# Two nearest prototypes sought in the products, distances on ScalarE, and one load for the last keys' products

## The reference, cut to what matters

```
x = x + tanh(g_xattn[1]) * L1_xattn(layernorm(x), ctx)         # 16 heads, softmax over 77 keys
xf = layernorm(x)
d2 = |xf|^2 + |p|^2 - 2 * (xf @ prototypes.T)                  # 32 prototypes
dists = sqrt(max(d2, 0))
w = softmax(-dists / t);  topw, topi = top_k(w, 2);  topw = topw / sum(topw)
for slot in 0, 1:
    h = B[topi[slot]] @ xf                                     # rank 16
    out += topw[slot] * (A[topi[slot]] @ h + bias[topi[slot]])
x = x + tanh(g_ffn[1]) * out
```

## Time and profile before

| | us |
|---|---|
| median of 3 runs | 3044.14 |
| lowest, highest | 3039.18, 3046.79 |
| the profiled execution, its own time | 3044.48 |
| its span, first to last instruction | 3042.8 |
| PE busy | 2739.6 (90%) |
| DVE busy | 2507.4 (82%) |
| POOL busy | 2089.8 (69%) |
| ACT busy | 1983.7 (65%) |

### The profile page before, as it was taken

How to read it: one execution, slowest core, us unless ns; L and a number is a source line. 1 busy time by engine, 2 the same in 40 slices (tenths; PEclk the granted TensorE clock), 3 DMA queues, 4 the chain that set the end, 5 groups by cost and what they waited for, 6 DMA issues and landing times.

```text
span 3042.8 us, 96434 instructions
## 1 busy us (share of the span) xinstructions
PE 2739.6 (90%) x31534; PEld 2166.8 (71%) x31534; DVE 2507.4 (82%) x6126; ACT 1983.7 (65%) x4683; POOL 2089.8 (69%) x2777
## 2 busy tenths in 40 slices
PE   4888896899999999689699999999989999999996
PEld 2444444677777777557578888888878888888885
DVE  6877776688888888675689999899989989999885
ACT  2666666687777877575466666666656666666663
POOL 3893000567666676544388888888888888888886
PEclk9999998899999999899899999999999999999998
DMA  5987566223233232631567766666776767766663
GB/s 152 364 337 294 235 254 256 76 81 93 77 90 84 80 93 76 220 117 41 121 142 158 158 147 149 140 145 150 145 137 149 141 144 149 147 150 145 145 132 78
DMA packets 638943, 455.55 MB, mean 150 GB/s; under 512 B 389760, under 2 KB 612592, under 8 KB 633648
## 3 DMA queue, kind: packets, MB, share of 16 engines
q1 hardware_dynamic: 618288, 402.31, 52.2%
q0 software_dynamic: 7328, 23.40, 2.5%
q10 hardware_dynamic: 12960, 25.23, 2.2%
HBM read 235.08 MB, written 148.83 MB: 126 GB/s over the span
## 4 chain that ended last, share of the span: by engine, by line
PE 32%; DVE 6%; issue 4%; POOL 3%; SPq 2%; ACT 2%; DMA 1%; DVEq 0%; POOLq 0%; ACTq 0%
PE banks L150 10%; PE banks L152 9%; PE banks L151 9%; PE banks L1416 2%; DVE a_near L1540 2%; PE banks L1401 2%; SPq L1058 1%; DVE a_probT_lo L1492 1%; ACT a_qT_hi L1234 1%; DVE a_pick L1627 1%; DVE a_rsum L1504 1%; DVE a_wtop L1567 1%; POOL a_pn L1154 1%; DMA a_xnT<-a_xn_parts 0%; DMA a_hwT<-a_hw_parts 0%
## 5 line engine op out<-in xcount | busy, mean ns | idle before, releaser
L1234 ACT ACTIVATE a_qT_hi<-banks 128x512 f16<-128x512 f32 x252 | 150.4, 597 | 540.8 <-PE banks L152 540.8
L383 POOL TENSOR_TENSOR a_probT_lo<-a_expT,a_probT_hi 128x512 f16<-128x512 f32 x256 | 291.4, 1159 | 218.5 <-ACT a_probT_hi L466 218.5
L459 ACT ACTIVATE a_expT<-banks,a_top,w_score_scale 128x512 f32<-128x512 f32 (+1 forms) x384 | 272.4, 709 | 152.5 <-PE banks L550 146.1
L1154 POOL TENSOR_TENSOR a_pn<-a_prob,a_rsum 128x1024 f32<-128x1024 f32 (+1 forms) x256 | 310.2, 1233 | 5.8 <-DVE a_rsum L1506 5.8
L150 PE MATMUL banks<-a_xnT,w_q_hi 128*128 128x256 f16 x1024 | 281.2, 275 | 15.0 <-DMA a_xnT<-a_xn_parts 13.2
L150 PE MATMUL banks<-a_vo_front,a_probT_hi 128*128 128x256 f16 x1024 | 279.8, 273 | 9.4 <-DVE a_probT_lo L1492 6.5
L152 PE MATMUL banks<-a_xnT,w_q_lo 128*128 128x256 f16 x1024 | 280.6, 274 | 0.0
L151 PE MATMUL banks<-a_xnT,w_q_hi 128*128 128x256 f16 x1024 | 280.6, 274 | 0.0
L152 PE MATMUL banks<-a_vo_front,a_probT_lo 128*128 128x256 f16 x1024 | 279.7, 273 | 0.0
L151 PE MATMUL banks<-a_vo_front,a_probT_hi 128*128 128x256 f16 x1024 | 279.6, 273 | 0.0
L1490 DVE TENSOR_TENSOR a_qT_lo<-banks,a_qT_hi 128x512 f16<-128x512 f32 x252 | 172.0, 683 | 77.9 <-ACT a_qT_hi L1234 77.7
(11 more groups left out here) (380 smaller groups left out, 10177.7 us busy)
## 6 DMA issues: line engine op xcount, KB each, us to landing
vo<-kv_vo_out SPq DMA_DIRECT2D x38, 2048.0 KB, 8.1
a_vo_front<-vo SPq DMA_DIRECT2D x128, 512.0 KB
kt<-kv_k_out ACTq DMA_DIRECT2D x9, 2560.0 KB, 14.9
a_k<-kt SPq DMA_DIRECT2D x64, 308.0 KB, 3.5
kv_raw_e<-in_L_ffn_w POOLq DMA_DIRECT2D x16, 1024.0 KB, 8.9
a_x<-in_x SPq DMA_DIRECT2D x64, 256.0 KB, 2.9
a_y<-in_x SPq DMA_DIRECT2D x64, 256.0 KB, 2.7
x<-a_y SPq DMA_DIRECT2D x64, 256.0 KB, 2.8
```

The source lines that it names most:

```text
L383: pool.tensor_tensor(probT[b][1][:, first:end, :], expT[b][:, first:end, :], probT[b][0][:, first:end, :], ALU.subtract).then_inc(prob_rea ...
L459: act.activation(expT[1 - h][0:rows, first:end, :], bank, ACT.Exp, bias=top[0:rows, 0:1], scale=weights["score_scale"][0:rows, 0:1]).then_ ...
L1154: last = pool.tensor_tensor(keys_of(pn[h]), e[:, :, first:end], rsum[h][:, :].unsqueeze(2).broadcast_to([P, H, end - first]), ALU.mult)
L1234: act.activation(out, bank[:, 0:cols].rearrange("p (c s) -> p c s", c=out.shape[1]), ACT.Copy, scale=scale)\
```

## The change: what it does

Part 1, the search. The eight largest and their places are now sought in the products `dots` themselves, so `near` and its instruction go. One number is set (`idle_top`) ahead of the search, to stand for the waits. The squared distance of the two found is made on ACT by a new step, `square_gaps`: `square = Relu(ysq - top)` of two columns, placed after `probT` 0 (and the query piece behind it) in the next half. POOL's first step in `top_weights` adds `TINY` to it where it changed a sign before, and waits for ACT's result. `ysq` gets four columns, so that a length lives until it is used two halves later.

Part 2, the load. The last 13 keys' products of a batch come in one transfer of 104 partitions and not in eight of 13. The row order of `vo_back` is now key by key (key, then pair of heads) and not pair by pair. So the second instruction of `normalise` writes `pn` in that order: it reads `prob` with a step of 154 numbers in its innermost run of 8, where it read 13 neighbouring numbers before.

```diff
-    VALUE_LOADS = 16 * (2 + MAIN)
+    VALUE_LOADS = 16 * (2 + 1)
...
-            for n in range(MAIN):
-                sp.dma_start(vo_back[p][n * BACK:(n + 1) * BACK, :, :, :], values_back(batch_at(i), n)).then_inc(vo_in[p], 16)
+            sp.dma_start(vo_back[p][:, :, :, :], values_back(batch_at(i))).then_inc(vo_in[p], 16)
...
-            for keys_of, first, end in ((first_keys, 0, FRONT), (last_keys, FRONT, KEYS)):
-                last = pool.tensor_tensor(keys_of(pn[h]), e[:, :, first:end],
-                                          rsum[h][:, :].unsqueeze(2).broadcast_to([P, H, end - first]), ALU.mult)
-            last.then_inc(pn_ready, 1)
+            pool.tensor_tensor(first_keys(pn[h]), e[:, :, 0:FRONT],
+                               rsum[h][:, :].unsqueeze(2).broadcast_to([P, H, FRONT]), ALU.mult)
+            pool.tensor_tensor(last_by_key(pn[h]), e[:, :, FRONT:KEYS].rearrange("p (n a) k -> p a k n", a=2),
+                               rsum[h][:, :].rearrange("p (n a) -> p a n", a=2).unsqueeze(2)
+                               .broadcast_to([P, 2, BACK, MAIN]), ALU.mult).then_inc(pn_ready, 1)
...
-            need(pool, top_used, t)
-            pool.tensor_tensor(dist[:, :], top[:, 0:2], numbers[:, 2:3].broadcast_to([P, 2]), ALU.mult).then_inc(top_used, 1)
+            need(pool, gap_ready, t + 1)
+            kept = pool.tensor_tensor(dist[:, :], square[:, :], numbers[:, 2:3].broadcast_to([P, 2]), ALU.add)
             pool.tensor_copy(topf[:, :], topi[:, 0:2]).then_inc(top_ready, 1)
-            need(pool, top_used, t + 1)
+            step(kept)
...
+        def square_gaps(t, h, u):
+
+            n = (TPB * u + h - 6) % LENGTHS
+            need(act, top_found, t + 1)
+            need(act, ysq_done, t + 1)
+            need(act, more_ready, t)
+            act.activation(square[:, :], top[:, 0:2], ACT.Relu, bias=ysq[:, n:n + 1], scale=-1.0).then_inc(gap_ready, 1)
...
                     if g == 0:
                         prep(0)
+                        if live(t - 6, NT):
+                            square_gaps(t - 6, h, u)
...
-            need(act, near_ready, t - 1)
-            act.activation(ysq[:, h:h + 1], inv2[:, :], ACT.Identity, scale=mv2[:, 1:2]).then_inc(ysq_done, 1)
+            act.activation(ysq[:, n:n + 1], inv2[:, :], ACT.Identity, scale=mv2[:, 1:2]).then_inc(ysq_done, 1)
...
+            need(dve, gap_ready, t)
             need(dve, dots_read, t + 1)
-            need(dve, ysq_done, t + 1)
-            nc.vector.tensor_scalar(near[:, :], dots[:, :], ysq[:, 1 - h:2 - h], -TINY, ALU.subtract, ALU.min)\
-                .then_inc(near_ready, 1)
-            need(dve, top_used, t)
-            hold(near_ready, t + 1)
-            nc.vector.max(top[:, :], near[:, :]).then_inc(top_found, 1)
+            nc.vector.memset(idle_top[:, :], 0.0)
+            nc.vector.max(top[:, :], dots[:, :]).then_inc(top_found, 1)
```

More of the change, by code:

```diff
@@ L743, in attention_ffn_phase @@
     LU = 2
+    LENGTHS = 4
     LAG = 8
@@ L747, in attention_ffn_phase @@
     HALVES = ((0, 0), (0, 1), (1, 0))
-    SUM_STEPS, TOP_STEPS = 2, 3
+    SUM_STEPS, TOP_STEPS = 2, 4
     sb = lambda n, s, d=FP32: ctx.enter_context(nc.sbuf_tensor(f"{name}_{n}", s, d))
@@ L792, in attention_ffn_phase @@
         sem("yn_ready"))
-    ln_log, ln_root, more_ready, first_weight = sem("ln_log"), sem("ln_root"), sem("more_ready"), sem("first_weight")
+    gap_ready, ln_log, ln_root, more_ready, first_weight = sem("gap_ready"), sem("ln_log"), sem("ln_root"), sem("more_ready"), sem("first_weight")
     ln2_inverse = sem("ln2_inverse")
     yn_hi, yn_lo, dots_read = sem("yn_hi"), sem("yn_lo"), sem("dots_read")
-    near_ready, top_found, topi_found, top_ready = (
-        sem("near_ready"), sem("top_found"), sem("topi_found"), sem("top_ready"))
-    top_step, top_used, wtops_ready, picked, wsel_ready = (
-        sem("top_step"), sem("top_used"), sem("wtops_ready"), sem("picked"), sem("wsel_ready"))
+    top_found, topi_found, top_ready = sem("top_found"), sem("topi_found"), sem("top_ready")
+    top_step, wtops_ready, picked, wsel_ready = (
+        sem("top_step"), sem("wtops_ready"), sem("picked"), sem("wsel_ready"))
     low_ready, hw_ready, hw_hi, hw_lo, wselT_hi, wselT_ready, out_ready = (
@@ L875, in gpsimd_numbers @@
         def gpsimd_numbers(self):
-            for n, number in enumerate((-0.5, 0.5, -1.0, 1.0)):
+            for n, number in enumerate((-0.5, 0.5, TINY, 1.0)):
                 pool.memset(numbers[:, n:n + 1], number).then_inc(numbers_set, 1)
@@ L952, in attention_ffn_phase @@
     ynT = [sb(f"ynT{p}", [P, 2 * DC, P], F16) for p in range(2)]
-    ysq = sb("ysq", [P, TPB])
-    dots, near = sb("dots", [P, NPROTO]), sb("near", [P, NPROTO])
+    ysq = sb("ysq", [P, LENGTHS])
+    dots, idle_top = sb("dots", [P, NPROTO]), sb("idle_top", [P, 1])
     top, topi, topf = sb("top", [P, 8]), sb("topi", [P, 8], U32), sb("topf", [P, 2])
-    dist, dgap, late, wtop = sb("dist", [P, 2]), sb("dgap", [P, 1]), sb("late", [P, 1]), sb("wtop", [P, 2])
+    dist, square, dgap, late, wtop = sb("dist", [P, 2]), sb("square", [P, 2]), sb("dgap", [P, 1]), sb("late", [P, 1]), sb("wtop", [P, 2])
     more, euler, decay = sb("more", [P, 1]), sb("euler", [P, 1]), sb("decay", [P, 1])
@@ L1340, in body @@
                                    scale=rstd2[:, 0:1]).then_inc(yn_ready, 1)
-                    length2(t - 4, h)
+                    length2(t - 4, h, u)
                     normed_high(t - 4, u, h, j)
@@ L1528, in prototype_products @@
             bank = full(i, ("low", h, 0))
-            need(dve, near_ready, t)
+            need(dve, topi_found, t)
             need(dve, low_ready, t * LU + 1)
@@ L1534, in prototype_products, with nearest_two @@
                 .then_inc(dots_read, 1)
-        def nearest_two(t, h):
+        def nearest_two(t):
+            need(dve, gap_ready, t)
             need(dve, dots_read, t + 1)
-            need(dve, ysq_done, t + 1)
-            nc.vector.tensor_scalar(near[:, :], dots[:, :], ysq[:, 1 - h:2 - h], -TINY, ALU.subtract, ALU.min)\
-                .then_inc(near_ready, 1)
-            need(dve, top_used, t)
-            hold(near_ready, t + 1)
-            nc.vector.max(top[:, :], near[:, :]).then_inc(top_found, 1)
+            nc.vector.memset(idle_top[:, :], 0.0)
+            nc.vector.max(top[:, :], dots[:, :]).then_inc(top_found, 1)
         def nearest_index(t):
             hold(top_found, t + 1)
-            nc.vector.max_index(topi[:, :], top[:, :], near[:, :]).then_inc(topi_found, 1)
+            nc.vector.max_index(topi[:, :], top[:, :], dots[:, :]).then_inc(topi_found, 1)
         def prepare(i, p, h, part):
@@ L1638, in body @@
                 if live(t - 5, NT):
-                    nearest_two(t - 5, h)
+                    nearest_two(t - 5)
                     nearest_index(t - 5)
@@ L2938, in flamingo_layers @@
     out_front = lambda i, a: out_rows[rows_of(i * KEYS, FRONT), a::2]
-    out_back = lambda i, n: out_rows[rows_of(i * KEYS + FRONT, KEYS - FRONT), n::H // 2]
+    out_back = lambda i: out_rows[rows_of(i * KEYS + FRONT, KEYS - FRONT)].rearrange("r (n a) k d -> (r n) a k d", a=2)
     with ExitStack() as ctx:
```

5 lines of the change are left out of this document (3 added, 2 removed).

## The result

| | before | after |
|---|---|---|
| median, us (5 runs each) | 3044.14 | 3076.27 |
| lowest to highest, us | 3039.18 to 3046.79 | 3064.51 to 3078.98 |
| profiled execution, us | 3044.48 | 3076.27 |
| its span, us | 3042.8 | 3074.6 |
| ratio to before, 95% interval | 1 | 1.0095 (1.0079 to 1.0111) |

The change makes the kernel slower by 0.95%; 3008 was forecast, with 3033 as the upper end. The forecast is wrong, in sign too.

What follows compares the result with a forecast made beforehand. The prediction took PE, 94% busy in the loop of layer 1, as the bound. Its terms, 31.7 + 10.5 + 4.7 - 10 = 36.9 us off 3044.48, gave 3008 us; range for 8 in 10, 2996 to 3033.

Steps and rivals of the forecast that it cites:

- the first term: On DVE in the second half, `near` leaves, the search starts about 1.2 us earlier, PE's `probT_lo` waits shrink by 31.7 us.
- 31.7 + 10.5 us of the sum: PE's gain in the loop: 31.7 us of `probT_lo` waits, and 10.5 us that recorded waits leave out.
- The second failed step: On ACT, `square_gaps` costs 0.2 us plus 0.1 us waiting for the search; 10 us given back in all.
- PE's wait for `probT` 2: PE's output product waits 0.13 us per body, 0.16 with a semaphore; 10 us given back over 62 bodies.
- The rival for slower: Search held by `xn_parts` in place of `near`, ACT 1.3 us later; 0.34 us per body lost, 3065 us; chance 7%.
- the first rival's case: ACT's new step and wait cost 0.6 us, PE waits 0.45 us per body for `probT` 2; 3026 us; chance 15%.
- the body of 23.2 us: Expected length of one loop body after the change, against 23.83 us before; staying at 23.8 would refute the prediction.
- the search at about 190 ns: On DVE, MAX8 was expected at about 195 ns also while POOL's `xn_parts` runs, within 0.2 us of `wsel`'s end.
- `hwT`'s waits: PE's eight waits in the loop for the transposed `hwT`, 4.7 us, were to go through earlier issue on SP.
- the scores' waits: PE's waits at line 1401 in the loop, 40.8 us in 62 times, were to stay about as before.
- SP's load cheaper: On SP, one issue of 104 rows was taken at 1 us, where eight take 8.47 us of a body.
- the wide read: POOL's second `pn` instruction goes from 550 ns to 0.7 us, between 0.5 and 1.05; nothing on the path.

Runs made afterwards that it cites:

- e4: The changed kernel with `wsel` made by a reduction over the two picks instead of a two-operand addition; 3030.49 us, 0.9945 of before.
- e11: The changed kernel with DVE's search put ahead of the weights, `wsel` still a two-operand addition; 3030.43 us, 0.9950 of before.
- e2: The kernel before with the load edit alone (one load, `pn` read with the wide step); 3051.71 us, 1.0009 of before.
- e3: The changed kernel with `pn`'s second instruction reading packed numbers and writing with the wide step; 3062.38 us, 1.0040 of before.
- e5: The changed kernel with both `wsel` by a reduction and `pn` written with the wide step; 3030.56 us, 0.9938 of before.
- e10: The kernel before with only ACT's exponential moved behind the third `probT_hi`; 3054.56 us, 1.0030 of before.
- e9: The changed kernel with `wsel` by a reduction and ACT's exponential moved behind the third `probT_hi`; 3056.54 us, 1.0035 of before.

## Why the prediction was wrong

The step that failed is the first term, as I put it: "In the second half 1.14 us and the gap of 0.13 behind it leave ... The search then starts about 1.2 us earlier". The reason for `near`'s 1.14 us was read rightly, POOL's `xn_parts`. The conclusion was not: I treated the hold as a cost of `near` that leaves with it. It is a cost of `xn_parts`, and falls on the next DVE instruction that can be held. I asked it of what comes behind (the search, the number set), and rightly found them free. I did not ask it of what stands in front. `wsel` had missed `xn_parts` by 0.03 us, a margin that a shift of 0.1 us uses up, and `quarter`, on `wtop` and the picks, gave one of 0.16 us. The search starts 0.22 us earlier and not 1.2. So nearly all of the 31.7 + 10.5 us of the sum was not there; PE's waits for `probT` 0 went from 26.8 to 22.5 us from 1500 to 2900 us, and not to nothing. A smaller slip: I priced all 33.6 us of the waits for `probT_lo` as waits for `probT` 0, but six of them, 6.5 us, were for `probT` 2.

The second failed step is the size of ACT's. I took 0.3 us for `square_gaps`: 0.2 for the step and 0.1 for the wait. The step was right (0.30 us long, 0.20 until the next begins), but the wait was 1.09 us, and the steps behind it came 1.39 us late. PE's wait for `probT` 2, 0.16 us in the forecast, was 0.73. Most of this follows from the first error, since the wait was computed from a search 1.2 us earlier. With that error out of the way, in e4, ACT is still 0.53 us late and not 0.3.

The rival for slower had this chain in full: the search ends late, ACT goes on 1.3 us later, 0.34 us per body, 3065. Measured: 1.39 us and 0.40 us per body. It had 7% because I tied it to the search itself being held, against which the rows spoke; the same effect by way of `wsel` stands in no rival. The condition was too narrow, the price was good for the body. The 11 us between 3065 and 3076 are 0.06 us a body, the loop's start 5.1 us later, and some 2 us behind the loop.

Even with the hold out of the way the forecast was 22 us too low: 3030 in e4 and e11, not 3008. In e4 ACT's step and its wait put ACT back by 0.53 us, and PE waits 0.53 us a body for `probT` 2, the first rival's case. In e11 that is cured, and the picks take the hold. So the body of 23.2 us was in none of the twelve runs; the best have 23.43 to 23.48.

Right were: the search at about 190 ns also under `xn_parts` (182 to 198 ns in e4; after the change itself the search comes only behind `xn_parts`, so that profile can't tell); `hwT`'s waits gone (4.7 us to none), though in e2 the load edit as a whole gains nothing; the scores' waits unchanged (38.1 against 40.8 us); SP's load cheaper, 0.44 us where I took 1; the wide read at 824 ns, within my 0.5 to 1.05, where I took 700. The estimate from the Trainium skill, GPSIMD Engine Reference, Performance pitfalls for Q7 kernels, that a wide read costs half as much again, was 0.83 us; this case's rows agree with it. That POOL has the time for it is right only without a hold: e3 gained some 14 us over after by making it cheaper, e5 nothing over e4.

One more rule stands behind the rows. `wsel` with two operands is held (774 ns), as a reduction it is not (357 ns), and in the kernel before `xn_parts`, started 0.03 us behind `wsel`, was itself the longer one (1.25 us against 1.16). The Trainium skill, SBUF — State Buffer, section Who interferes with whom, says that a VectorE instruction with two inputs in SBUF contends with a GpSimd instruction that reads SBUF, that one in a two-port mode contends for the pair of ports they share, which the first to issue has for its whole length, and that a reduction on trn2 never contends. It counts `tensor_scalar`, which is what `near` and `pick` are, among the operations that can enter a two-port mode; that they were in one no run here shows, only that they are held. The rows of `wsel` and `xn_parts` agree. Its line that issue order decides who blocks is what the forecast should have been held against.

## What to carry to other kernels

When an instruction is slow because another engine holds it, ask which of its neighbours, in front and behind, would be held in its place once the timing moves by 0.1 us; taking out the victim doesn't take out the hold. Make the victim of a kind that wasn't held here (a reduction; one operand alone is not enough, since `near` and the picks read one tile each and are held) or put it in an order in which the holder can't start yet. Each brought 0.5% here, where removing the victim cost 1%. And a step that newly waits for a late result belongs on an engine behind which nothing urgent is queued; a price worked out from another term of the same forecast falls together with it.

## What the hardware showed that I had not expected

- On `near` and `wsel` together the hold keeps its size as it moves: 419 ns a half on `near` before, 240 + 177 in e2, 421 on `wsel` in e10. What `wtop` and the picks lose ahead of them comes on top and does not: they take 0.94, 1.05 and 1.11 us in a second half of these three.
- A pair of 0.29 us picks can be stretched to 1.81 us by two POOL instructions in a row (e9).
- A wide step costs POOL on the read side (824 against 550 ns for 208 numbers) and next to nothing on the write side (574 ns, e3).
- One issue over 104 rows takes SP 0.44 us, eight over 13 rows each 8.47 us. So the price doesn't grow with the rows; why one over 13 rows costs more, 1.06 us, than one over 104 is open.
